# Cross-attention with a routed feed-forward layer: one product with V moved from slot 1 to slot 2, next to the ones pass

## The reference

```python
Q  = split_heads(layernorm(x), 16) * 32 ** -0.5
Kh, Vh = split_heads(k_mem, 16), split_heads(v_mem, 16)
logits = einsum('bhqd,bhkd->bhqk', Q, Kh) + b + MASK * (1 - valid)
out = einsum('bhqk,bhkd->bhqd', softmax(logits), Vh)
x = x + tanh(g_xattn) * merge_heads(out)
x = x + tanh(g_ffn) * moe_ffn(layernorm(x))     # 8 experts, top 2 of them per row
```

## Time and profile before

| what | value |
|---|---|
| median of 3 runs | 1841.51 us (1840.8 to 1842.31) |
| the profiled execution | 1838.65 us |
| its span | 1836.9 us |
| TensorE busy | 1718.4 us (94%) |
| VectorE busy | 1364.6 us (74%) |
| GpSimd busy | 1224.8 us (67%) |
| ScalarE busy | 1190.2 us (65%) |
| L828, products with V | 2048 instructions, from 86.4 to 1281.0 us |
| L842, ones pass | 1040 instructions, from 101.4 to 1284.5 us |

### The profile page before, as it was taken

The page is one execution under the profiler, slowest core; times in us unless marked ns, Lnnn a source line. Parts: engine busy times, 40 slices in busy tenths (PEclk is TensorE's granted clock), DMA queues, the critical chain, the costliest instruction groups (busy, mean ns, idle before and its releaser), DMA issues. The chain is left out here.

```text
span 1836.9 us, 33094 instructions
## 1 busy us (share of the span) xinstructions
PE 1718.4 (94%) x9714; PEld 1038.6 (57%) x9715; DVE 1364.6 (74%) x3007; ACT 1190.2 (65%) x2049; POOL 1224.8 (67%) x1395
## 2 busy tenths in 40 slices
PE   1699999999999999999999999999499999999997
PEld 1344545555555555555555555553378887878876
DVE  4677878878778788887887887773666776767765
ACT  4267677676776767767677676767256666666664
POOL 1257667585675857758577576654368888888886
PEclk9999999999999999999999999999599999999999
DMA  5979899898998989889889897974468888887784
GB/s 118 173 129 188 155 181 170 144 197 162 172 178 136 209 151 172 186 128 210 151 170 187 128 207 106 186 128 145 128 134 170 154 160 160 177 155 150 153 164 75
DMA packets 173099, 291.45 MB, mean 159 GB/s; under 512 B 38014, under 2 KB 42110, under 8 KB 172976
## 3 DMA queue, kind: packets, MB, share of 16 engines
q1 hardware_dynamic: 138704, 219.88, 62.1%
q0 software_dynamic: 32960, 67.68, 18.5%
q10 hardware_dynamic: 1312, 2.38, 0.8%
HBM read 127.09 MB, written 71.63 MB: 108 GB/s over the span
## 5 line engine op out<-in xcount | busy, mean ns | idle before, releaser
L1157 DVE TENSOR_REDUCE bank<-bank 128x1 f32<-128x512 f32 x1024 | 696.0, 690 | 255.0 <-PE bank L906 246.9
L751 ACT ACTIVATE prob<-bank 128x512 f32<-128x512 f32 x1024 | 593.1, 597 | 355.2 <-PE bank L894 354.1
L655 POOL TENSOR_TENSOR prob<-prob 128x512 f32<-128x512 f32 x252 | 315.8, 1294 | 319.0 <-PE bank L828 319.0
L894 PE MATMUL bank<-stB,stack_a_then_w_hi 100*128 100x512 f32 x1024 | 476.0, 466 | 16.0 <-ACT prob L751 13.7
L906 PE MATMUL bank<-stack_a_then_w_hi,stB 98*128 98x512 f32 x1024 | 423.1, 415 | 35.0 <-DMA stack_a_then_w_hi<-regrouped_then_w 19.7
L894 PEld LDWEIGHTS bank<-stB,stack_a_then_w_hi 100*128 100x128 f32 x1024 | 193.2, 189 | 248.4 <-ACT prob L751 176.3
L659 POOL TENSOR_TENSOR prob<-prob 128x512 f32<-128x512 f32 x252 | 315.5, 1295 | 0.0
L828 PE MATMUL bank<-prob,vin 128*32 128x512 f32 x2048 | 272.7, 605 | 0.7 <-ACT prob L751 0.7
L1429 POOL DMA_INDIRECT out_dram<-yout,scatter_ids x144 | 227.8, 1582 | 50.2 <-issue 38.1
L906 PEld LDWEIGHTS bank<-stack_a_then_w_hi,stB 98*128 98x128 f32 x1024 | 197.8, 193 | 84.7 <-DVE bank L1157 40.0
L1402 POOL DMA_INDIRECT rows_in<-xn_rows,gather_ids x152 | 181.6, 1195 | 71.5 <-issue 43.7
(11 more groups left out here) (202 smaller groups left out, 2160.7 us busy)
## 6 DMA issues: line engine op xcount, KB each, us to landing
stB<-regrouped_then_w SPq DMA_DIRECT2D x192, 256.0 KB, 5.7
stack_a_then_w_hi<-regrouped_then_w SPq DMA_DIRECT2D x183, 256.0 KB, 6.5
x_k_then_w<-in_x_dram SPq DMA_DIRECT2D x16, 1024.0 KB, 7.9
x_k_then_w<-in_ctx_dram SPq DMA_DIRECT2D x16, 1024.0 KB, 11.0
vin<-in_ctx_dram SPq DMA_DIRECT2D x16, 1024.0 KB, 8.7
xres<-in_x_dram SPq DMA_DIRECT2D x16, 1024.0 KB, 6.4
out_dram<-xres SPq DMA_DIRECT2D x16, 1024.0 KB, 7.2
xn_rows<-xn SPq DMA_DIRECT2D x60, 256.0 KB, 5.4
```

The costliest lines, as they stand in the source:

```text
L655: pool.tensor_tensor(first[:, j, :], first[:, j, :], more[:, j, :], ALU.add).then_inc(s_acc, 1)
L751: act.activation(prob_of(st, 0, u)[:, j, :], psS[j % 2][:, :], ACT.Exp).then_inc(s_exp, 1)
L894: pe.matmul(psS[j % 2][:, :], stA[0:100, g, j, kt * P:(kt + 1) * P], stB[0:100, g, j, :], start=True, stop=True).then_inc(s_qk, 1)
L1157: dve.tensor_reduce(mx[:, s // 4, s % 4:s % 4 + 1], psM[s % 2][:, :], AX.X, ALU.max).then_inc(s_mx, 1)
```

## The change

The call of `values` for the last key block moves from slot 1 to slot 2, directly ahead of the ones pass. No instruction is added or removed.

```diff
                         if j == 1 and u > 0 and st.on(0):
                             values(st, 0, u - 1)
-                        if s == 1 and st.on(-1):
+                        if s == 2 and st.on(-1):
                             values(st, -1, NT - 1)
-                        if s == 2 and st.on(-1):
                             sums(st, -1)
```

## The result

The changed kernel takes 1849.4 us (median of 5 runs, 1847.47 to 1851.08) against 1840.8 us of the kernel before in the same comparison (5 runs, 1839.59 to 1842.31): a ratio of 1.0046, 95% interval 1.0034 to 1.0058. It is slower by 8.6 us. The forecast was 1849.5 us, 8 us slower than 1841.5. The profiled execution has a span of 1845.7 us, 8.8 more than before.

A forecast was written before the change was run, and what follows sets the result against it. TensorE's arrival at slot 3 was taken as the bound. Four steps lose 0.59 us, fifteen rounds 8.9, three other steps save 1.0: 8 us longer, 1849.5 us against the 1841.51 median, range 1840 to 1858.

The forecast's parts named there:

- the sum: Whole attention: 8.9 us lost in fifteen rounds of four steps, 1.0 saved in three others, 8 us longer.
- the three steps: Steps 1, 62 and 63, outside the four-position pattern: each saves up to 0.33 us, 1.0 in all.
- What bounds the kernel: TensorE's arrival at slot 3 decides the rest of the step; time lost or won before it counts in full.
- The merged run: Slot 2: 24 instructions cost 2.72 us instead of 2.86; with fewer switches, slot 1 to 3 drops 0.33 to 3.82.
- the bounds for the third eight: Last eight instructions of the merged run: between 0.86 and 1.00 us, 0.86 taken; 1.00 would add 8.4 us.
- The lost cover: Slot 2: M(2) waits for R(0), starting 0.06 us behind its end, the run 0.42 later; four steps 0.59 us longer.
- the full saving: Rival: R(0) does not hold M(2), so 20.8 us go, giving 1820.7; chance 0.11 with partial holds.
- Drain of a mode change: Switches around 32-column work: changing tiling mode drains TensorE, seen as extra tenths; by this rule alone the change wins.
- Weight loads: M(2) in slot 2: its load waits at the semaphore, no longer hidden; 0.10 us in each of 60 steps, 6 us.
- The rival within 0.2%: Slot 2: M(2)'s load stays hidden or R(0) comes a tenth earlier; 2 us longer, 1843.5; chance 0.16.

The follow-up runs named there:

- both_slot1: Changed kernel with the merged run of 24 (product with V and ones pass) moved to slot 1 behind M(1); 1841.03 us against 1841.68 for the kernel before.
- run_before_m2: Changed kernel with the run of 24 placed between the logits of slot 2 and M(2); 1825.61 us against 1841.68 for the kernel before.
- both_slot1_copy1: On top of both_slot1, ScalarE's copy of the finished bank moved to slot 1 too; 1825.45 us against 1840.6 for the kernel before.
- m2_early: Kernel before with M(2) moved to slot 1, behind M(1) and ahead of the product with V, nothing merged; 1885.37 us against 1841.68.
- two_maxima: Changed kernel with two places for the maxima, negated and split behind R(0), TensorE's order untouched; 1825.99 us against 1841.68 for the kernel before.
- two_maxima_lg: On top of two_maxima, VectorE's copy of the route scores also moved behind R(0); 1824.61 us against 1840.6 for the kernel before.

## Why the prediction was right

The mechanism held, and not only the number. That 1849.5 and 1849.4 agree to a tenth is luck all the same: the sum is 1 us short (see the three steps below), and the kernel before came in 0.7 us lower in this comparison than in the one that the forecast starts from.

*What bounds the kernel.* TensorE's arrival at slot 3 decided the rest of the step in the changed kernel, as forecast: from slot 3 to slot 6 it takes 3.39 us on average over steps 2 to 61, before and after, and from there to slot 1 of the next step the difference is 0.01 us. It need not be so: in both_slot1 the stretch from slot 3 to slot 6 takes 3.61 us, since the late exponential of slot 3 holds the logits of slot 5, and in run_before_m2 and both_slot1_copy1 the wait of M(5) takes part of the gain back there. From slot 6 to slot 1 of the next step all seven kernels agree with the kernel before to 0.01 us on average.

*The merged run.* 2.72 us were put down for 24 instructions; the rows show 0.88 + 1.83 = 2.71. The lower end of the bounds for the third eight, which the forecast took, was right. The saving of 0.33 us is real, and four experiments collect most of it.

*The lost cover.* M(2) 0.06 (here 0.05) behind the end of R(0), the run 0.42 (0.44) behind M(2): both transferred from slot 13 to slot 2 as read. R(0) itself ends 2.37 us behind the start of M(15) on average over the steps, before and after, so nothing melted, and the full saving could not land. m2_early showed the same wait with nothing merged, and two_maxima showed the saving with the order on TensorE untouched. Together they say that wait and merge are separate terms that add up.

*Drain of a mode change.* The Trainium skill says ("TensorEngine Tiling (Array Packing)", section "Tiling Modes") that a change of tiling mode drains TensorE. By that rule alone the change could only win, and it lost. The half of the sum that goes with the rule came out: the rows show 0.1 us at a switch each way and about 0.14 at the run's end. That this time is a drain, and not only a weight load that isn't pulled ahead across the switch, no run here separates. The other half is what the 32-column work hid where it stood.

*Weight loads.* In the changed kernel the load of M(2) starts with its matmul in every step from 2 to 61, and in the kernel before 0.23 us ahead of it. In none of the eight traces, over these steps, does the load of an M start earlier than 0.05 us behind the end of the maximum that it waits for. The run starts 0.43 us behind M(2) on average instead of 0.32, so this was worth 6 to 7 us of the 8.6.

*The three steps outside the pattern.* Here the sum was off: it gave up to 0.33 us to each, 1.0 in all. Between slot 1 and slot 3, step 1 saves 0.30 us, step 62 only 0.03 and step 63 only 0.09, 0.4 in all. The rows of step 63 in the changed kernel, TensorE and then its weight loads, say why:

```profile
1274.34 0.98 PE L894 MATMUL bank<-stB,stack_a_then_w_hi 100*128 100x512 f32 x2 [0.45 <-ACT prob L751]
1275.25 1.07 PE L828 MATMUL bank<-prob,vin 128*32 128x512 f32 x8
```

```profile
1274.83 0.19 PEld L894 LDWEIGHTS bank<-stB,stack_a_then_w_hi 100*128 100x128 f32 x1 [0.30 <-ACT prob L751]
```

Steps 62 and 63 have no M, so little stands between the two logits, and those of slot 2 wait for the exponential of slot 0. In step 63 they start 0.05 us behind its end, where in the kernel before it was 0.99, with the product with V as cover, and in step 35 of the changed kernel it is 0.27, as forecast. They stand 0.49 us behind those of slot 1, and the run 0.42 behind them, which with its 2.71 makes 3.62 us instead of 3.71. With this, and 0.62 instead of 0.59 in four steps, the sum would have been 9 us.

*A chance.* The rival within 0.2% rested on the load of M(2) or a tenth in R(0). two_maxima_lg shows that the load becomes almost free if R(0) ends 0.11 us ahead of M(2); but then the wait is gone as well. In the changed kernel R(0) ends 0.45 us behind M(2)'s turn, and no run shows a product that waits and has its load hidden, so nothing in the rows speaks for this rival.

## What to carry to other kernels

Before two blocks of work are joined, ask what each of them hides where it stands: find the next instruction behind the gap, the semaphore it waits for, and when that comes, and compare it with the new start. Here a saving of 0.33 us in a step stood against a wait of 0.3 to 0.5 that had been covered for nothing, and the tenth behind it; joining the blocks between the logits and M(2), so that the cover stays, turned a loss of 9 us into a gain of 16. And price a wait with what follows it: here the weight load behind the semaphore added a tenth of a microsecond.

## What the hardware showed unexpectedly

A wait that ended just before a matmul's turn wasn't free here: with R(0) done 0.11 us ahead of the start of M(2) (two_maxima_lg) the instruction behind M(2) started 0.36 us later instead of 0.32, with R(0) done 0.05 us ahead of the start 0.43 (two_maxima). And a single full-width matmul between two 32-column runs cost 0.42 us (m2_early), while two of them in the same place cost 0.65.
